# Layer 0's cross attention: the values of the preceding unit placed directly behind a unit's scores

## The reference, cut to what matters

```
q  = (layer_norm(x) @ w_q)          # 8 x 64 tokens, 16 heads of 64
kv = context @ w_kv                 # 8 x 512 keys, k and v for 16 heads of 64
scores = q * SCALE @ k^T            # per sequence and head: 64 x 512
attn   = softmax(scores)
out    = attn @ v                   # per sequence and head: 64 x 64
x      = x + (out @ w_out + b_out) * tanh(gate)
```

## Time and profile before

| | us |
|---|---|
| median of 3 runs | 1763.58 (1763.0 to 1765.14) |
| profiled execution, span | 1759.1 |
| PE busy in it | 1715.7 (98%) |
| DVE, ACT, POOL busy | 910.5, 716.4, 238.3 |
| stage in which the units run | about 64 to 495 of the span |

### The profile page before, as it was taken

The page is one execution under the profiler, slowest core; times in us unless marked ns, Lnnn a source line. Parts: engine busy times, 40 slices in busy tenths (PEclk is TensorE's granted clock), DMA queues, the critical chain, the costliest instruction groups (busy, mean ns, idle before and its releaser), DMA issues.

```text
span 1759.1 us, 28411 instructions
## 1 busy us (share of the span) xinstructions
PE 1715.7 (98%) x11211; PEld 1315.8 (75%) x11211; DVE 910.5 (52%) x2029; ACT 716.4 (41%) x1564; POOL 238.3 (14%) x317
## 2 busy tenths in 40 slices
PE   7999999999999999999999999999999899999997
PEld 5677777777757666555999986777758587999997
DVE  4234344434346686523756564665564864455543
ACT  3333333333324436422655554555445442243432
POOL 0100000000003202422111031211101221121112
PEclk9999999999999999999999999999999999999999
DMA  6011010102042003025999961111231312788983
GB/s 248 25 73 48 25 48 25 49 25 96 1 156 96 1 1 144 23 99 214 375 390 390 384 200 60 37 37 31 79 144 35 155 59 96 317 329 325 327 326 94
DMA packets 43666, 245.87 MB, mean 140 GB/s; under 512 B 5786, under 2 KB 6290, under 8 KB 20481
## 3 DMA queue, kind: packets, MB, share of 16 engines
q1 hardware_dynamic: 31248, 215.91, 32.2%
q0 software_dynamic: 7664, 19.68, 4.0%
q10 hardware_dynamic: 4608, 8.33, 1.2%
HBM read 228.29 MB, written 16.13 MB: 139 GB/s over the span
## 4 chain that ended last, share of the span: by engine, by line
PE 92%; DVE 3%; issue 2%; DMA 1%; ACT 1%; POOL 1%; SPq 0%; POOLq 0%; DVEq 0%; ACTq 0%
PE bank L639 29%; PE bank L259 22%; PE bank L265 4%; PE bank L782 3%; PE bank L3284 3%; PE bank L810 3%; PE bank L1971 3%; PE bank L1973 3%; PE bank L1972 3%; PE bank L736 2%; PE bank L2773 2%; PE bank L1473 2%; PE bank L729 2%; PE bank L1157 2%; PE bank L1530 1%
## 5 line engine op out<-in xcount | busy, mean ns | idle before, releaser
L639 PE MATMUL bank<-split 128*128 128x512 f32 x2196 | 539.7, 398 | 0.8 <-ACT arena L665 0.8
L639 PEld LDWEIGHTS bank<-split 128*128 128x128 f32 x2196 | 401.9, 188 | 130.8 <-issue 21.7
L259 PE MATMUL bank<-arena,weights 128*128 128x128 f32 (+1 forms) x1992 | 244.7, 282 | 11.8 <-DMA weights<-in_L_xattn_w_kv 8.8
L259 PEld LDWEIGHTS bank<-arena,weights 128*128 128x128 f32 x1992 | 232.6, 192 | 25.2 <-issue 13.5
L753 DVE TENSOR_REDUCE small<-bank 128x1 f32<-128x512 f32 x64 | 43.9, 686 | 166.1 <-PE bank L729 166.1
L790 ACT COPY normed<-bank 128x512 f32<-128x512 f32 x128 | 68.9, 591 | 125.7 <-PE bank L782 125.7
L671 DVE COPY arena<-bank 128x512 f32<-128x512 f32 x76 | 52.4, 689 | 111.8 <-PE bank L639 111.8
L665 ACT COPY arena<-bank 128x512 f32<-128x512 f32 x76 | 44.6, 587 | 149.2 <-PE bank L639 116.0
L265 PE MATMUL bank<-weights,arena 128*128 128x512 f32 x224 | 102.9, 610 | 0.9 <-issue 0.9
L772 ACT ACTIVATE normed<-bank,small 128x512 f32<-128x512 f32 x64 | 44.1, 690 | 124.0 <-DVE small L755 123.7
L3390 DVE SCALAR_TENSOR_TENSOR arena<-bank,cols,arena 128x128 f32<-128x128 f32 x96 | 30.5, 349 | 114.5 <-issue 67.1
(11 more groups left out here) (397 smaller groups left out, 2915.8 us busy)
## 6 DMA issues: line engine op xcount, KB each, us to landing
weights<-in_L_ffn_re_w SPq DMA_DIRECT2D x62, 1024.0 KB, 8.2
weights<-in_L_w SPq DMA_DIRECT2D x20, 1408.0 KB, 11.0
arena<-in_ctxT SPq DMA_DIRECT2D x24, 1024.0 KB, 4.8
arena<-in_L_w SPq DMA_DIRECT2D x12, 1408.0 KB, 8.9
weights<-in_L_w_full SPq DMA_DIRECT2D x10, 1280.0 KB, 10.4
weights<-in_L_ffn_sw SPq DMA_DIRECT2D x9, 1024.0 KB, 4.9
expert_out<-arena ACTq DMA_DIRECT2D x31, 256.0 KB, 8.2
arena<-in_L_w_full SPq DMA_DIRECT2D x6, 1280.0 KB, 10.2
```

What stands on the lines that cost most here:

```text
L259: s = pe.matmul(out, w[:, k, j0:j0 + m], rhs(k), start=(k == 0), stop=(k == KT - 1))
L639: s = pe.matmul(bank[:, :], still, moving, start=(n == 0), stop=(n == len(order) - 1))
```

## The change

In layer 0, for units 1 to 29, `values_tensor(n-1)` is called right behind `scores_tensor(n)`, ahead of F, and no longer between F and S. Units 0, 30 and 31, and layer 1, keep their order. No instruction is added or taken away; DVE's, ACT's, POOL's and SP's programs are the same.

```diff
             for n, c, u, first, second, third, splits in self.plan:
+                adjoin = self.layer == 0 and 1 <= n < beside
                 self.scores_tensor(pe, n)
+                if adjoin:
+                    self.values_tensor(pe, n - 1)
                 self.queries_tensor(pe, self.queries_beside(c, u))
                 for g in first:
                     self.kv_tensor(pe, *g)
@@
-                if n >= 1:
+                if n >= 1 and not adjoin:
                     self.values_tensor(pe, n - 1)
                 for g in second:
                     self.kv_tensor(pe, *g)
```

## The result

The changed kernel takes 1756.7 us (median of 20 runs) where the kernel before, timed beside it, takes 1763.8. The ratio is 0.9956, with a 95% interval of 0.9946 to 0.9967, that is 5.8 to 9.5 us less. The forecast was 1757.2 and a gain of 6.4.

What follows compares the result with a forecast made beforehand. PE, busy throughout the stage, was taken as the bound. Saving 29 x 0.22 = 6.4 us turns the span of 1759.1 into 1752.7; with 4.5 around it, 1757.2 us, range 1754.4 to 1760.8.

Steps and rivals of the forecast that it cites:

- What bounds the stage: Layer 0's units, 64 to 495 us: PE is busy for all 431.00 us, so its sequence alone counts.
- The size: 29 units of layer 0, each 0.22 us shorter (14.34 to 14.12): 6.4 us saved in all.
- the joined row of F and S: F and S as 24 matmuls in a row: 5.60 us, as in unit 0, instead of 5.82, saving 0.22 a unit.
- the borders one by one: V's two borders between F and S: 0.08 us in and 0.11 out, 0.19 a unit removed.
- What lies around the span: Time outside the profiled span: 1763.58 less 1759.1 is 4.5 us, added to the new span of 1752.7.
- The new border from the scores to V: Between two small forms in each moved unit: costs the same as scores to F, inside the scores' 1.02 us.
- The rival without a border: Scores to V costs no border: 0.08 to 0.09 us more saved a unit, 1754.6 us; chance 0.08.
- Only the way in is saved: Borders around V: every weight load stays bare, so only 29 x 0.08 = 2.3 us saved, 1761.3; chance 0.04.
- The waits that move: V, softmax and copies in layer 0's units: all waits already met, with 5.7 us of room for V; no cost.
- Slower by the clock in the stage: 2.10 us of small tiles lowers PE's clock in layer 0's units, 1.7 us a dip, up to 1806; chance 0.04.
- Lost behind the stage: After layer 0's units: two more clock dips take back 3.4 us (1760.6), or all 6.4 goes (1763.6); chance 0.10.

Runs made afterwards that it cites:

- the two comparisons: The changed kernel timed twice against the kernel before: ratio 0.9956 the first time, 0.9964 when run once more.
- the second profile of the kernel before: Profile from the kernel before timed once more against itself, nothing changed: ratio 1.0006 (0.9994 to 1.0019).

## Why the prediction was right, point by point

**What bounds the stage.** Right: PE has no wait in it before or after, and 5.81 us of the stage went with 29 times 0.20.

**The size.** The sum was right in kind and 0.6 us too large. The term that was mis-sized is the joined row of F and S. Unit 0's 5.60 was taken, and 5.62 was measured; the changed kernel's own unit 0 still has 5.60 (66.04 to 71.64). The prediction's other estimate, 0.19 from the borders one by one, came nearer to the measured 0.20 than the 0.22 that it chose. Unit 0 enters the row from the scores, units 1 to 29 enter it from V, and with V behind the turn the row is entered from the scores and takes 5.60 (208.13 to 213.73). V ahead of the scores has 5.62 too, though, where the row is entered from the scores; so the last block alone doesn't explain it, and two small blocks in a row may. What makes these 0.02 us was not found.

That 1756.7 lies only 0.5 from the forecast 1757.2 is partly luck: the units give 5.8, 6.4 were forecast, and the two comparisons gave 7.1 and 5.7 between their medians.

**What lies around the span.** Misread, without harm to the forecast. The 4.5 us take one execution's span from the median of other runs. A run's time is 1.8 us above its own span here (1759.57 and 1757.8 in the changed kernel, 1762.28 and 1760.5 in the second profile of the kernel before). By this estimate the first profile of the kernel before shows an execution of about 1760.9 us, below the lowest of its 20 runs (1761.37). The forecast starts from 1763.58 and takes 6.4 off, so it holds without this term.

**The new border from the scores to V.** Priced at no difference, by the earlier trace rows. Right: scores to V is 1.02 us, as scores to F was. The rival without a border (0.93) is refuted.

**Only the way in is saved.** Refuted: the row of 24 would then take 5.7 us. The rule of the Trainium skill quoted with it (TensorE: Matmul & The Clock Gate, Part 3, "What overlaps and what doesn't"), that a weight load overlaps matmuls in flight only if it goes to other rows of the array, doesn't hold inside these rows, where loads of 188 ns on all 128 rows run under matmuls that follow each other every 235 ns. Behind V a load does lie bare. These are the first two weight loads of S in the kernel before, and its matmuls from the second on, in narrow windows of the unit of the earlier trace rows:

```profile
210.68 0.19 PEld L639 LDWEIGHTS bank<-split 128*128 128x128 f32 x1
...
210.79 0.19 PEld L639 LDWEIGHTS bank<-split 128*128 128x128 f32 x1
...
211.02 0.63 PE L639 MATMUL bank<-split 128*128 128x512 f32 x2
```

The first load starts at 210.68 together with its matmul, the second at 210.79, 0.23 ahead of its own.

Another page of the Trainium skill, TensorEngine Tiling (Array Packing), "Key Properties", states that a change of the tiling mode drains TensorE. The runs here agree in that every change of form costs something: 0.08 us for a way in from a row of groups, about 0.11 for a way out, 0.17 from the turn to V, and no less between two small modes (scores to V takes as long as scores to F). How much of this is a drain and how much the bare load was not separated.

**The waits that move.** Right. Normalising ends at 209.68 and the turn starts at 213.04, 3.4 us of room (3.3 was forecast); the turned probabilities are ready at 214.80 and V starts at 220.47; ACT's copy of F now runs at 210.51, later relative to the scores, and nobody waits for it. The rows of DVE and ACT, for the unit shown first:

```profile
209.19 0.49 DVE L762 TENSOR_SCALAR normed<-normed,small 128x512 f32<-128x512 f32 x1
```

```profile
210.51 0.59 ACT L665 COPY arena<-bank 128x512 f32<-128x512 f32 x1 [1.56 <-PE bank L639]
...
213.72 1.08 ACT L790 COPY normed<-bank 128x512 f32<-128x512 f32 x2
```

**Slower by the clock in the stage.** Refuted: with 2.10 us of small forms in a row in 29 units, the clock is 1.00 in the window above, and in each window of 40 us between 64 and 489, where a dip of 1.7 us would show as 0.96.

**Lost behind the stage.** In the median no. The first two profiled spans differ by only 1.3 us (1759.1 and 1757.8), though the stage lost 5.81, because the profiled execution of the kernel before lies 2.9 below that kernel's median (about 1760.9 by the estimate above, against 1763.8), and that of the changed kernel 2.9 above its own (1759.57 against 1756.7). The last section has where the rest stands. The forecast allowed for this with the clock's dips, and the medians don't show it.

## What to carry to other kernels

Where TensorE bounds a stage and shows no waits, look at starts instead of busy time: a block of small array tiles cost about 0.2 us more between full-tile matmuls than beside another small block (0.20 to 0.23 in the two stages measured here), so put small blocks side by side, in whatever order the waits allow. Look for a place in the trace where the new sequence already occurs (here the first unit, which lacks one block); it measures the change as a whole and checks the sum of the parts (0.22 and 0.19 here, against a measured 0.20). One profiled span is a poor measure of a gain of a few us; compare the stage inside the two profiles, and the medians outside.

## What the runs showed of the hardware that was not expected

**The clock's dips don't fall in the same places in every profile.** One window of the kernel before and of the changed one, from their first profiles; the columns end with the granted clock, the DMA share and GB/s:

```profile
1310.00:1330.00 20.00, 19.05 (x89) 13.59 (x88) 9.49 (x21) 14.41 (x28) 0.00 (x0) 1.00 0.12 50
```

```profile
1310.00:1330.00 20.00, 19.23 (x72) 12.59 (x72) 7.32 (x16) 12.88 (x25) 0.00 (x0) 0.91 0.01 5
```

The stretch from 1310 to 1330 us has no dip in either profile of the kernel before (1.00 and 1.00), and 0.91 in both profiles of the changed kernel: 1.8 us of full-speed time (20 times 0.09). The kernel with V behind the turn, as slow as the kernel before, has 0.83 there, and the one with V ahead of the scores, which saves as much as the change, has 1.00, so the dip isn't the change's own. What decides where a dip falls was not found.

**The start varies too.** The same 8 matmuls of L259 at the head of the kernel took 5.10 us in the first profile of the kernel before and 6.19 in that of the changed one, before any changed instruction, and most of the 1.5 us by which the changed kernel reached unit 0 later came from them:

```profile
8.76 5.10 PE L259 MATMUL bank<-arena,weights 128*128 128x512 f32 x8 [8.76 <-DMA weights<-in_L_xattn_w_kv]
```

```profile
8.79 6.19 PE L259 MATMUL bank<-arena,weights 128*128 128x512 f32 x8 [8.79 <-DMA weights<-in_L_xattn_w_kv]
```

In the second profiles both kernels took 5.31 there. Why it varies was not tested. So of the 5.81 us that the stage lost, 1.5 were given back ahead of it in this one execution, and the changed kernel is 4.3 ahead at the first block of the output projection (493.51 less 489.20). It is 2.8 ahead both at the first and at the last scores of layer 1 (1072.4 less 1069.6, 1297.5 less 1294.7), and 1.3 at the end. The last 1.5 went behind layer 1's scores, where the dip between 1310 and 1330 costs 1.8. The 1.5 between 494 and 1072 are explained only in part: the clock from 780 to 830 is 0.94 before and 0.93 afterwards, a difference of 0.5.
